# First batch of an attention and FFN kernel: its inverse root by ScalarE's square root and one Newton step, one token tile normalised on ScalarE, and the splits of the weights put in another order

## What is computed

```python
xn = (x - mean(x)) / sqrt(var(x) + 1e-5)              # over the 256 features
q, k, v = xn @ Wq.T, xn @ Wk.T, xn @ Wv.T             # 16 heads of 16
w = softmax(q k^T / 4 + causal mask)
s = (w v) @ Wo.T
gate = silu(qlinear(xn, wq_gate, s_gate))             # 704 hidden, integer weights less 128, scaled
up = qlinear(xn, wq_up, s_up)
g = silu(qlinear(gate * up, wq_down, s_down))
out = x + s * g
```

## Time and profile before

| | us |
|---|---|
| median of 3 runs (lowest, highest) | 310.57 (309.98, 311.3) |
| the profiled execution | 309.06 |
| its span, first to last instruction | 307.3 |
| TensorE busy in the span | 275.4 (90%) |
| VectorE busy | 228.0 (74%) |
| ScalarE busy | 177.5 (58%) |
| GpSimd busy | 137.0 (45%) |

### The profile page before, as it was taken

One profiled execution on the slowest core, in us unless ns is written; L12 is line 12 of the kernel. 1 busy time (PEld: TensorE's weight loads), 2 busy tenths in 40 slices (PEclk: granted clock), 3 DMA queues, 4 the chain that ended last, 5 costly groups with the idle time before them and its releaser, 6 DMA issues.

```text
span 307.3 us, 5488 instructions
## 1 busy us (share of the span) xinstructions
PE 275.4 (90%) x2024; PEld 189.0 (62%) x2024; DVE 228.0 (74%) x384; ACT 177.5 (58%) x256; POOL 137.0 (45%) x241
## 2 busy tenths in 40 slices
PE   0797996789899999999999999999999999999972
PEld 0585673567456566797755566887655566775531
DVE  5883968575899879748799988558698987679424
ACT  3645448743475888333666898243576767344750
POOL 5007634711277845301586864101666564115361
PEclk9999999999999999999999999999999999999998
DMA  7647579179307404277314720286406520001302
GB/s 269 202 117 205 162 141 232 36 199 144 130 0 138 72 4 136 58 189 150 126 34 85 125 73 1 80 202 134 139 0 118 94 70 4 0 0 38 105 2 69
DMA packets 21470, 31.39 MB, mean 102 GB/s; under 512 B 2612, under 2 KB 10420, under 8 KB 21444
## 3 DMA queue, kind: packets, MB, share of 16 engines
q1 hardware_dynamic: 21028, 30.39, 41.2%
q10 hardware_dynamic: 416, 0.66, 0.6%
HBM read 20.19 MB, written 10.49 MB: 100 GB/s over the span
## 4 chain that ended last, share of the span: by engine, by line
PE 63%; DVE 16%; DMA 7%; ACT 4%; issue 4%; SPq 3%; POOL 2%; ACTq 0%
PE ps L674 13%; PE ps L676 10%; PE ps L675 10%; PE ps L862 9%; PE ps L843 8%; PE ps L800 6%; DVE ps L1368 3%; DVE mx L1376 3%; DMA sdb<-in_sd 3%; PE ps L870 2%; DMA qk_scratch<-xr 2%; ACT pt L1069 2%; DVE mx L1371 2%; DVE mx L1373 1%; POOL zbuf L1177 1%
## 5 line engine op out<-in xcount | busy, mean ns | idle before, releaser
L1069 ACT ACTIVATE pt<-ps 128x1024 f32<-128x1024 f32 x80 | 81.8, 1026 | 39.8 <-PE ps L843 34.5
L1225 POOL TENSOR_SCALAR_AFFINE_SELECT pt<-pt 128x256 f32<-128x256 f32 (+1 forms) x112 | 47.7, 441 | 113.7 <-ACT pt L1069 113.3
L1368 DVE TENSOR_TENSOR ps<-ps,tri 128x512 f32<-128x512 f32 (+1 forms) x72 | 42.6, 591 | 33.5 <-PE ps L800 33.4
L862 PE MATMUL ps<-pt,vt 128*17 128x256 f32 (+3 forms) x512 | 43.0, 437 | 1.8 <-POOL pt L1225 1.6
L843 PE MATMUL ps<-qp,kp 50*128 50x512 f32 (+3 forms) x256 | 39.8, 370 | 4.1 <-ACT pt L1069 3.5
L1371 DVE TENSOR_REDUCE mx<-ps 128x2 f32<-128x1024 f32 x32 | 39.1, 1225 | 3.5 <-PE ps L814 2.5
L800 PE MATMUL ps<-kp,qp 48*128 48x512 f32 (+3 forms) x256 | 35.6, 336 | 5.5 <-DMA kp<-qk_scratch 2.7
L1186 POOL TENSOR_TENSOR hid<-hid 128x512 f32<-128x512 f32 (+1 forms) x24 | 30.8, 1283 | 19.6 <-ACT hid L1014 12.4
L843 PEld LDWEIGHTS ps<-qp,kp 50*128 50x128 f32 x256 | 20.2, 184 | 27.8 <-issue 15.4
L1193 POOL TENSOR_TENSOR hl<-hid,hh 128x512 fp32r<-128x512 f32 (+1 forms) x24 | 30.8, 1284 | 13.4 <-ACT hh L1024 13.3
L1373 DVE TENSOR_REDUCE mx<-ps 128x2 f32<-128x768 f32 x32 | 30.7, 959 | 2.4 <-PE ps L814 1.4
(11 more groups left out here) (143 smaller groups left out, 568.9 us busy)
## 6 DMA issues: line engine op xcount, KB each, us to landing
qk_scratch<-hid SPq DMA_DIRECT2D x24, 256.0 KB
qp<-qk_scratch SPq DMA_DIRECT2D x14, 256.0 KB, 4.8
kp<-qk_scratch SPq DMA_DIRECT2D x14, 256.0 KB, 6.5
qp<-qk_scratch SPq DMA_DIRECT2D x18, 128.0 KB, 5.2
kp<-qk_scratch SPq DMA_DIRECT2D x18, 128.0 KB, 6.9
xr<-in_x SPq DMA_DIRECT2D x4, 512.0 KB, 3.6
out<-xr SPq DMA_DIRECT2D x8, 256.0 KB, 2.2
xin<-in_x SPq DMA_DIRECT2D x3, 512.0 KB, 7.0
```

What stands on the lines that cost most here:

```text
L862: mm = nc.tensor.matmul(ps[32 * a:32 * a + HD + 1, BZ, j * P:], vt[:, j, GH * g + a, :], pt[:, k, c:c + T - j * P], start=(j == 0), stop=( ...
L1069: nc.scalar.activation(pt[:, 2 * kk:2 * kk + 2, :], ps[:, base:base + 2, :], ACT.Exp, scale=SCALE).then_inc(exp_done, 1)
L1225: mm = nc.gpsimd.affine_select(out=diag, in_=diag, compare_op=ALU.is_ge, fill=0.0, base=0, pattern=[[0, diag.shape[1]], [1, P]], channel_m ...
L1368: nc.vector.tensor_tensor(diag, diag, mask, ALU.add).then_inc(tri_added, 1)
```

## The change

The bit trick and three Newton rounds (11 small VectorE instructions) give way to a square root on ScalarE, a reciprocal on VectorE and one Newton round. VectorE then computes the negative product of mean and root (`shf`), normalises tiles 0 to 2, and ScalarE normalises tile 3 as scale times x plus `shf`. The rounding copy of Wq, Wk, Wv is made in two parts, the v columns behind tile 3. The rounding copies of the gate and up weights move behind the two `xh` copies and behind chunk 1 of `chunk_hi`. VectorE waits for the v columns' copy before it makes their low part. The program order on the other engines stays.

```diff
+        sqrt_done, first_shift = map(sem, ("sqrt_done", "first_shift"))
...
+            def split_qkv_hi(cols):
+                nc.scalar.copy(wh[:, :, cols], raw_qkv.rearrange("p (k n) -> p k n", k=KD)[:, :, cols]).then_inc(wh_done, 1)
+
+
+            act_e.wait_ge(ln_step, TT + 1)
+            nc.scalar.activation(nw[:, 1, :], nw[:, 0, :], ACT.Sqrt).then_inc(sqrt_done, 1)
             act_e.wait_ge(wqkv_loaded, 32)
-            nc.scalar.copy(wh[:].rearrange("p k n -> p (k n)"), raw_qkv).then_inc(wh_done, 1)
+            split_qkv_hi(slice(0, 2 * D))
+            act_e.wait_ge(first_shift, 1)
+            nc.scalar.activation(xn[:, TT - 1, :], xin[:, TT - 1, :], ACT.Identity, scale=nw[:, 1, TT - 1:],
+                                 bias=shf[:, TT - 1:]).then_inc(xn_done, 1)
+            split_qkv_hi(slice(2 * D, 3 * D))
+
             def split_gu_hi(w):
...
-            split_gu_hi(0)
             split_x(0, 0)
             split_x(0, 1)
+            split_gu_hi(0)
+            chunk_hi(0, 0)
+            chunk_hi(0, 1)
             split_gu_hi(1)
-            for c in range(4):
-                chunk_hi(0, c)
+            chunk_hi(0, 2)
+            chunk_hi(0, 3)
...
             def first_root():
-                ln(nc.vector.tensor_scalar(nwi[:, 0, :], v.bitcast(I32), 1, None, ALU.logical_shift_right))
-                ln(nc.vector.tensor_scalar(y.bitcast(I32), nwi[:, 0, :], -1.0, MAGIC, ALU.mult, ALU.add))
+
+                dve.wait_ge(sqrt_done, 1)
+                ln(nc.vector.reciprocal(y, y))
...
             first_root()
-            for _ in range(NEWTON):
-                newton()
-            for i in range(TT):
+            newton()
+            nc.vector.scalar_tensor_tensor(shf[:], mv[:, :, 0], -1.0, y, ALU.mult, ALU.mult).then_inc(first_shift, 1)
+            for i in range(TT - 1):
                 normalise(0, i)
             dve.wait_ge(wh_done, 1)
...
             for k in range(KD):
                 split_x(0, k)
+            dve.wait_ge(wh_done, 2)
             split_qkv_lo(slice(2 * D, 3 * D))
```

## The result

The changed kernel takes 308.86 us (median of 20 runs, 307.31 to 310.08). The kernel before, in 20 runs on the same chip beside it, takes 310.28 us (308.96 to 313.17). The ratio is 0.9955, with an interval of 0.9936 to 0.9974: faster by 1.4 us, between 0.8 and 2.0 us. A later repetition, twelve runs, gave 308.12 us and 0.9930 (0.9899 to 0.9961). The profiled execution took 307.77 us, its span 306.0 us.

The account below looks back on a forecast made before the run. Up to 29 us, when q and k are stored was taken to decide, not TensorE's work. Root 0.92 and tile 0.35 us give 1.27 us at the transposes, 1.1 us at the q store: 309.4 us, range 308.4 to 310.8 us.

Parts of the forecast that it names:

- The root: VectorE's start: new root 1.29 us in place of 2.18 us, normalisation at 7.35 instead of 8.27 us, 0.92 us gained.
- The tile on ScalarE: Normalisation: three tiles on VectorE save 0.35 us; ScalarE's tile ends at 8.3 us, 0.1 us before VectorE; transposes at 8.53 us.
- rival 5: Tile 3 hangs on the weights' landing; a landing at 9.6 us delays transposes and gives 312.2 us; chance 0.05.
- Chunk 0: VectorE, held by the late gate copy, reaches the low part at 14.17 us; q store at 14.88 us, 1.10 us gained.
- The k store and the landing: SyncE issues the k store at about 16.2 us, 1.25 us earlier; landing takes q's smaller gain, 1.1 us.
- First scores: TensorE's first scores start at 27.9 instead of 29.04 us, and later stages keep the gain of 1.1 us.
- The table load: Second load before Tanh on ScalarE takes 1.28 us, Tanh 0.5 us late, covered by TensorE's 2.1 us wait.
- The sum: Whole kernel: 1.1 us off, profiled execution 309.06 to 307.95 us, median to 309.4 us, 0.36%.
- Rival 1: Later stages add: k store's 1.25 us counts fully or root is cheaper, and a later transfer gains; 308.8 us; chance 0.22.
- Rival 2: TensorE's clock step stays at its time, slowing chunk 1's matmuls; 0.6 us lost, 309.9 us; chance 0.14.
- Rival 3: q and k transfers land as before although issued 1.1 us earlier, held by other loads; 310.6 us; chance 0.09.
- rival 4: Table load outlasts its cover because POOL's chain behind Tanh falls behind; 0.5 of 1.1 us lost, 310.0 us; chance 0.03.

Follow-up runs that it names:

- old_root: Changed kernel with the old bit trick and three Newton rounds, so one table load; 309.98 us, ratio 1.0011.
- gate_copy_first: Changed kernel with the gate weights' copy back ahead of the two `xh` copies; 308.13 us, ratio 0.9941.
- tile_first: Changed kernel with ScalarE's tile 3 ahead of the copy of Wq and Wk, so not waiting for the weights; 308.97 us, ratio 0.9955.
- chunks_first: Changed kernel with the gate weights' low part (`gl`) on VectorE behind the low parts of chunks 0 and 1; 307.37 us, ratio 0.9911.
- root_only: Kernel before with the new root alone, four tiles on VectorE and the old order of copies; 307.47 us, ratio 0.9943.
- chunks_first_filled: Changed kernel with `gl` behind the low parts of chunks 0 and 1, plus twelve unread matmuls on TensorE; 308.28 us, ratio 0.9944.
- before_filled: Kernel before with twelve short unread matmuls in TensorE's gaps of batch 0; 309.06 us, ratio 0.9969.
- two_more_loads: Changed kernel with one-column Exp and Sqrt ahead of the first Tanh, so three table loads there; 308.99 us, ratio 0.9968.

## Why the prediction came true

The forecast was 309.4 us, range 308.4 to 310.8 us; measured were 308.86 us, a gain of 1.42 us against the same chip's 310.28 us where 1.1 us was said. Of the 0.54 us by which the median is below the forecast, 0.29 us are the kernel before, which three runs had put at 310.57 us and twenty put at 310.28 us. Point by point:

**What bounds.** Right. The first scores, and ahead of them the stores of q and k, set the gain: old_root, whose stores are as late as before, gains nothing that can be told, and every kernel with early stores gains. That later stages keep what the first scores gain is borne out by gate_copy_first, whose trace has no fall before 303 us: its down product starts at 64.17 us, 1.32 us earlier than before. In the changed kernel's own trace it starts at 65.01 us, 0.48 us earlier, where 64.4 us was forecast; the fall of the clock stands in front of it.

**The root.** 1.29 us was taken for the new one and 7.35 us for `normalise`; measured are 7.21 us. The square root took the 0.20 us taken, the reciprocal 0.18 us; the hand-overs cost 0.03 and 0.11 us, 0.14 us in all as taken. The 0.14 us by which it was early are half the start (5.99 instead of 6.06 us) and half `shf`, which held VectorE for 0.08 us and not 0.15 us.

**The tile on ScalarE.** Here a size was off, and one of the prediction's own signs of being wrong came up: ScalarE's tile ended after VectorE's. "The weights land at 6.64 us" was read as a property of the kernel; in this execution they landed at 7.05 us. The copy that waits for them starts at 6.50 to 7.07 us in the traces that have it first. VectorE was through at 8.26 us (forecast 8.40), but ScalarE's tile ended at 8.62 us (8.3), and the transposes started at 8.77 us (8.53). This is the mechanism of rival 5, at 0.4 us of lateness instead of 1.3 us. In tile_first and gate_copy_first they start at 8.56 and 8.53 us. At the first scores this costs no more than the last read varies: tile_first's transposes and stores are earlier and its first scores are not.

**Chunk 0.** Right in kind: VectorE reaches chunk 0 only after `gl`, so a part of the gain is lost there. The late copy of the gate weights has little to do with it: VectorE was free for `gl` at 12.64 us and not at 12.3 us, and the copy ended at 12.71 us. VectorE reached chunk 0 at 14.42 us (forecast 14.17), and the q store was issued at 15.13 us (14.88), 0.85 us before that of the earlier trace rows and not 1.10 us. The high part of chunk 0 was ready 0.28 us before that; chunks_first, where the low part follows the high part at once, confirms that `gl` is what holds it.

**The k store and the landing.** The k store was issued at 16.65 us (16.2), a gain of 0.80 us. That k lands by q's store and not by its own, which I took as the smaller gain, is borne out: in all traces the first read of k follows the first read of q by 2.9 to 3.4 us, whether k's store went out 1.3 us behind q's (root_only) or 2.1 us (chunks_first_filled).

**First scores.** Forecast 27.9 us, measured 27.85 us, and the repetition's 27.77 us. The gain of 1.19 us is more than that of the stores, 0.80 to 0.85 us, which I had named as a sign against me. The first read of k gained 0.97 us; the remaining 0.2 us is in the last read, which takes 2.5 to 3.1 us in these traces with no order that I can see. So that 27.85 us meets the forecast of 27.9 us is luck in part: the stores fell 0.25 and 0.45 us short of it, and the transfers made it up.

**The table load.** Right: Tanh came at 19.93 us, which is the end of chunk 3's high part, 18.62 us (forecast 18.17), and the load with no gap. The drain of about 1380 ns, stated by the Trainium skill's "ScalarE: Activation LUTs", What ACT_TABLE_LOAD costs, does not appear in the four switches before the first Tanh of these two kernels; the measurement decides. The cover was smaller than said but real: TensorE still waits 1.4 us for `kp` where about 2 us was forecast, so one load costs nothing at the first scores; three did. The late up weights and the late Tanh cost TensorE waits of 0.3 us for `u` and 0.2 us for `hid`, near the 0.6 us said, in work that ends 1.4 us before `kp` lands.

**The sum.** 1.1 us was too small, by a term that the prediction did not have. After TensorE's last work the changed kernel needs 3.36 us from the issue of the last store to the end of the span (302.64 to 306.0 us), the kernel before 4.13 us (303.17 to 307.3 us). The issues in the timelines of before and after (start, us):

```profile
303.17 0.92 SPq L620 DMA_DIRECT2D out<-xr  x2
```

```profile
302.64 0.92 SPq L621 DMA_DIRECT2D out<-xr  x2
```

The queues' rows on the pages of before and after differ in one packet:

```profile
q14 instruction: 10, 0.08, 0.1%
```

```profile
q14 instruction: 9, 0.07, 0.1%
```

In before that tenth packet, 8 KB of instructions, travels at 305.4 to 305.7 us, among the last output stores. All three kernels with the old root (before, old_root, before_filled) have it there; all eleven with the new root, seven VectorE instructions shorter, have nine packets and none there. The stores land in 2.6 to 2.7 us with it and in 2.2 to 2.3 us without.

The term is there in every trace, but the split of the gain is not settled. The two traces without a fall before 303 us, before and gate_copy_first, differ by 1.35 us at TensorE's last matmul and by 0.85 us behind it, 2.2 us in all: there the whole gain of the first scores arrives. The changed kernel gains 1.5 and 1.8 us at equal clock and 1.57 us with the filler, which with 0.8 us at the tail leaves 0.7 to 1.0 us for the start, less than the 1.1 us forecast. The profiled execution came out at 307.77 us where 307.95 us was forecast, and that is luck: at TensorE's last matmul it was 0.5 us ahead, for the fall of the clock, and the tail added 0.8 us.

The Trainium skill's "Runtime: NRT & Kernel Launch", Instruction fetch mechanics, says that code comes in blocks and that crossing to the next is mostly hidden; if this packet is what holds the last stores up, it is one that is not hidden. That seven instructions less keep VectorE from fetching once more, and that the fetch is what lengthens the tail, is argued from these coincidences and wasn't tested: a kernel with the new root and seven idle instructions would do it.

**The rivals.** Rival 1 (308.8 us) comes nearest to the median, but not by its reasons: the k store gained 0.80 us and not 1.25 us, and no later transfer got a gap; what came on top lies behind the last store's issue. Rival 2, the clock's rise staying in place, was half there: the transposes moved by 1.03 us and the rise by 0.50 us (14.69 to 14.19 us). It read the granted clock as 1.00 from the start; the traces have no clock record before the rise, the queries count such a stretch as full, and the matmuls in it follow each other in 0.43 us, the pace of the 1.2 GHz level. In the traces of all kernels the rise lies anywhere from 12.30 to 14.69 us, in the two of the changed kernel at 14.19 and 13.28 us. That it differs from run to run, and with it the number of slow matmuls, agrees with the Trainium skill's "TensorE: Matmul & The Clock Gate", The HAM clock gate. But the larger part of the clock was not in my rivals at all: falls, mostly after TensorE's gaps, at 24 to 60 us. Rival 3 is out, since the first scores moved by 1.19 us; rival 4 is out by two_more_loads, where even three loads cost 0.75 to 1.1 us in all.

## What to carry to other kernels

A shorter start pays in full only if nothing else stands in front of the first result that others wait for; here it was VectorE's `gl`, and moving one call gave 0.3 to 0.6 us more at equal clock where taking a tile off VectorE gave nothing that can be told. Compare kernels at the same granted clock, or fill the gaps, before believing differences of a few tenths of a per cent; and put fillers only where the engine would really be idle, looking again each time the gap moves. A landing time read from one execution is a sample: where a step is to hang on it, leave it a margin. And look at the end of the span as well as at the place that was changed: 0.8 us of this gain may lie there.

## What the runs showed of the hardware

- TensorE's clock fell to half behind gaps of 1.3 to 2.8 us in some executions and not in others, and stayed there for 3.4 to 10.2 us; once it fell with no gap over 0.45 us ahead of it. Each 0.01 of mean granted clock went with 0.97 us. Twelve matmuls that nobody reads, in the gaps, brought the mean clock of the kernel before from 0.982 to 0.993 and its time down by 0.9 us (0.2 to 1.7 us).
- A table switch on ScalarE cost 1.3 us from the load's start to the next instruction's, nine times of nine where that instruction waited for nothing else (seven traces); in the four others it waited another 0.15 us for TensorE.
- A square root of 128x4 on ScalarE takes 0.20 us and the way from VectorE to it and back 0.14 us, so a round trip costs less than two instructions of VectorE at their pace of 0.20 us.
- An 8 KB instruction fetch in the midst of the last output stores goes with 0.7 to 0.85 us more of tail, in three traces against eleven; that it is the cause was not tested.
